# Two edge columns of passes 1 to 3, one of pass 4 and one of the last scatter moved by single-row transfers

## What is computed

```
edge_index = stack([src, dst])
h = relu(layernorm(x)); x = x + RGAT(relu(RGAT(h, W1..)), W2..)   # passes 1 and 2
h = relu(layernorm(x)); x = x + GAT(h)                           # pass 3
h = relu(layernorm(x)); x = x + RGCN(h, edge_weight)             # pass 4
h = relu(layernorm(x)); x = x + GINE(h, edge_attr)               # last layer
# attention: alpha = leaky(q[etype,dst] + k[etype,src]); softmax over the edges of a dst;
#            out[dst] = sum softmax * xw[etype, src]
# GINE:      message[e] = relu(h[dst[e]] + edge_attr[e]); out[src[e]] += message[e]
```

## Time and profile before

| | us |
|---|---|
| median of 3 runs | 36401.83 (36386.37 to 36415.52) |
| profiled execution, span from its first to its last instruction | 22678.7 |
| pass 1, from POOL's first gather to DVE's start on the last chunk | 447 to 4473 |
| pass 2, the same | 4779 to 8740 |
| pass 3, the same | 9049 to 13010 |
| pass 4, POOL's first to last gather | 13248 to 17207 |
| last layer's scatter, POOL's first to last | 17530 to 21634 |

### The profile page before, as it was taken

One profiled execution on the slowest core, in us unless ns is written; L12 is line 12 of the kernel. 1 busy time (PEld: TensorE's weight loads), 2 busy tenths in 40 slices (PEclk: granted clock), 3 DMA queues, 4 the chain that ended last, 5 costly groups with the idle time before them and its releaser, 6 DMA issues.

```text
span 22678.7 us, 201879 instructions
## 1 busy us (share of the span) xinstructions
PE 5315.0 (23%) x30665; PEld 3876.7 (17%) x30665; DVE 10606.0 (47%) x9480; ACT 5421.1 (24%) x4707; POOL 16413.3 (72%) x17069
## 2 busy tenths in 40 slices
PE   2000000020000001222222266666662222222201
PEld 1000000010000001222222255555552000000001
DVE  2444444324444443556566668888884111111167
ACT  1222222222222222111111132222221211121175
POOL 7777777677777776777777767777776777777733
PEclk9999999999999999666666655555555666666655
DMA  6333333332222222222222232222222222222164
GB/s 203 95 98 101 95 98 98 88 97 76 70 75 70 72 73 46 54 54 58 54 57 55 52 87 56 52 56 52 56 52 61 84 76 76 76 80 80 66 235 162
DMA packets 782414, 1839.84 MB, mean 81 GB/s; under 512 B 380834, under 2 KB 415306, under 8 KB 720302
## 3 DMA queue, kind: packets, MB, share of 16 engines
q0 software_dynamic: 544128, 569.36, 13.8%
q10 hardware_dynamic: 88736, 721.35, 8.1%
q1 hardware_dynamic: 148622, 541.43, 6.7%
HBM read 1007.43 MB, written 929.12 MB: 85 GB/s over the span
## 4 chain that ended last, share of the span: by engine, by line
POOL 55%; issue 24%; SPq 12%; DMA 3%; DVE 2%; PE 2%; ACT 1%; POOLq 0%; DVEq 0%; ACTq 0%
POOL region L652 41%; POOL by_src L742 12%; SPq L615 9%; SPq L613 3%; DMA region<-by_src 2%; DMA row_list<-row_lists 1%; POOL q_rel L713 1%; SPq L614 1%; PE ps L1207 1%; DVE region L1567 1%; DVE region L1538 0%; PE ps L1168 0%; POOL h_edge L725 0%; PE ps L1209 0%; POOL q_one L713 0%
## 5 line engine op out<-in xcount | busy, mean ns | idle before, releaser
L652 POOL DMA_INDIRECT region<-table,idx x12688 | 11972.1, 944 | 3941.9 <-issue 3873.2
L742 POOL DMA_INDIRECT by_src<-region,idx x3224 | 3122.7, 969 | 1007.9 <-issue 1001.5
L1950 DVE TENSOR_TENSOR region<-ps,region 128x248 f32<-128x248 f32 (+1 forms) x156 | 74.4, 477 | 3958.0 <-DMA region<-table,idx 1967.5
L1216 PE MATMUL ps<-ident,region 128*68 128x128 f32 (+1 forms) x3 | 1.3, 444 | 8044.9 <-DVE region L2013 8044.9
L1767 DVE TENSOR_TENSOR region<-ps,region 128x2048 bf16<-128x2048 f32 x833 | 1845.8, 2216 | 18.2 <-DVE region L1761 8.0
L870 ACT COPY region<-region 128x4216 f32<-128x4216 f32 (+1 forms) x156 | 1182.2, 7579 | 2477.7 <-DVE region L1996 2477.7
L1112 PE MATMUL ps<-region 98*128 98x128 f32 x6448 | 1657.9, 438 | 323.3 <-DVEq L1833 192.8
L1533 DVE CAST region<-src 128x62 f32 (+1 forms) x52 | 11.7, 224 | 3463.8 <-DMA by_src<-region,idx 3463.6
L1207 PE MATMUL ps<-region,ident 128*128 128x512 f32 (+1 forms) x832 | 809.5, 1062 | 3141.2 <-DVE region L1538 3141.2
L1112 PEld LDWEIGHTS ps<-region 98*128 98x128 f32 x6448 | 1455.9, 330 | 410.7 <-DVEq L1833 269.7
L1905 DVE TENSOR_TENSOR_SCAN region<-region,ps 128x1008 f32<-128x1008 f32 x624 | 1382.9, 2244 | 10.7
(11 more groups left out here) (291 smaller groups left out, 16216.1 us busy)
## 6 DMA issues: line engine op xcount, KB each, us to landing
sums<-region ACTq DMA_DIRECT2D x104, 2232.0 KB
region<-table SPq DMA_DIRECT2D x13312, 0.3 KB
sums<-region ACTq DMA_DIRECT2D x104, 1984.0 KB, 11.1
region<-table,idx POOLq DMA_INDIRECT x12688
region<-table SPq DMA_DIRECT2D x6656, 0.3 KB
region<-table SPq DMA_DIRECT2D x6656, 0.2 KB
sums<-region ACTq DMA_DIRECT2D x52, 2046.0 KB
region<-by_src SPq DMA_DIRECT2D x52, 2015.0 KB, 9.6
```

Of the source, the lines that this page charges most:

```text
L652: pool.indirect_dma_start(out=to, out_offset=None, in_=table, in_offset=bass.IndirectOffsetOnAxis(ap=index, axis=0)).then_inc(s, 16)
L742: pool.indirect_dma_start(out=by_src, out_offset=bass.IndirectOffsetOnAxis(ap=idx[:, b, j:j + 1], axis=0), in_=MSG[:, b, j, :], in_offset= ...
```

## The change

- In passes 1 to 3 the last **two** columns of each chunk (256 rows) go by single rows, and POOL gathers 60. SP fetches rows 0 to 143 of these 256, ACT rows 144 to 255, from a function `fetch_rows` of its own. ACT does so inside `score_chunk` for the chunk after the one that it works on: it asks for its part of the list at the start, fetches 80 rows after the mask at line 1001 and before its wait for the scores, and 32 rows after the exponentials and before `store_sums`. All 112 rows of the first chunk come before the loop.
- Pass 4 keeps one column by rows, by SP alone, and 61 by POOL.
- The lists hold byte offsets instead of row numbers (DVE multiplies them once, near the start), and the row DMAs are addressed in bytes (`U8`), so that no register instruction is left between two of them. 32 registers are loaded at a time (`RUN`), not 16. SP asks for the lists of both chunks of a turn at its start.
- The zeros over `h_edge` are written in quarters, one in each of the four passes, after each chunk.
- In the last layer POOL scatters 61 columns; SP stores the 128 rows of column 62, one DMA each, with row numbers that are written to DRAM as `rank_lists` when the layer begins. These keep the register instruction. SP does this between its loads: the loads of chunk c+1 come before the rows of chunk c.

```diff
+ROWED = {0: 2, 1: 2, 2: 2, 3: 1}
-RUN = 16
+RUN = 32
+SP_ROWS = 144
+FEWER = 32
+GROUPS_2 = [(0, 64), (64, 128), (128, SP_ROWS), (SP_ROWS, 208), (208, ROWS)]
...
@@ sync, at the start (one column of src and of edge_type before)
+            for j in range(2):
+                sp.dma_start(list_src[:, of], a["src"].rearrange(...)[:, :, J - 2 + j]).then_inc(loaded, 16)
+                sp.dma_start(list_type[:, of], a["edge_type_8"].rearrange(...)[:, :, J - 2 + j]).then_inc(loaded, 16)
...
@@ sync, last layer
+                    def load_edges(i, b):
+                        sp.wait_ge(he_t, i * 8 + (4 * b + 4))
+                        sp.dma_start(HE[...], he[...]).then_inc(he_in[b], 16)
+                        sp.wait_ge(edge_sum, i * (2 * NS) + (NS * b + 1))
+                        sp.dma_start(EA[...], ea[...]).then_inc(ea_in, 16)
+                    def send_rows(i, b, back):
+                        nth = b - 2 * back
+                        sp.dma_start(row_list[b:b + 1, 0:P], rank_lists[bass.ds(i * 2 + nth, 1), :]).then_inc(list_in[b], 16)
+                        sp.wait_ge(idx_ready, i * 2 + ((CH + 2) * len(SUMMED) + nth + 1))
+                        sp.wait_ge(xs_ready, i * (2 * NS) + (NS * nth + NS + 2))
+                        sp.wait_ge(list_in[b], i * 16 + 16 * (CH // 2 * len(SUMMED) + 1 - back))
+                        for p0 in range(0, P, RUN):
+                            sp.load(indices, row_list[b:b + 1, p0:p0 + RUN])
+                            for k, row in enumerate([sp.snap(r) for r in indices]):
+                                p = p0 + k
+                                sp.dma_start(by_src[bass.ds(row, 1), :], MSG[p:p + 1, b, J - 1, :]).then_inc(msg_rows[b][p // 64], 16)
+                    load_edges(0, 0)
+                    sp.dma_start(rank_lists.rearrange("c p -> p c"), src8[:, J - 1:EPP:J]).then_inc(lists_out, 16)
+                    sp.wait_ge(lists_out, 64)
+                    load_edges(0, 1)
+                    send_rows(0, 0, 0)
+                    with sp.Fori(1, CH // 2) as i:
+                        load_edges(i, 0)
+                        send_rows(i, 1, 1)
+                        load_edges(i, 1)
+                        send_rows(i, 0, 0)
+                    send_rows(CH // 2, 1, 1)
...
@@ sync, passes 1 to 4
+                mine = (0, SP_ROWS) if ROWED[l] == 2 else (P, ROWS)
...
+                        for k0 in range(mine[0], mine[1], RUN):
+                            n = min(RUN, mine[1] - k0)
+                            sp.load(indices[0:n], row_list[b:b + 1, k0:k0 + n])
+                            for k, row in enumerate([sp.snap(r) for r in indices[0:n]]):
+                                sp.dma_start(row_place(l, b, k0 + k), row_bytes(l, row)).then_inc(...)
-                        if l == CONV1:
-                            sp.dma_start(he[:, bass.ds(i * (2 * J * D) + b * J * D, J * D)], zeros_d).then_inc(big_zero, 16)
+                        w = J * D // QUARTERS
+                        sp.dma_start(he[:, bass.ds(i * (2 * J * D) + (b * J * D + l * w), w)], zeros_d[:, 0:w]).then_inc(big_zero, 16)
...
@@ gpsimd
-                            for j in range(J):
+                            for j in range(J - 1):
...
-                        for j in range(JP):
+                        for j in range(gathered_columns(l)):
...
@@ scalar, passes 1 to 3
+                    ask_rows(0, 0)
+                    rows_begin(0, 0)
+                    fetch_between(0, SP_ROWS, ROWS)
...
+                        if more:
+                            ask_rows(i + b if b else i, 1 - b)
                         act.copy(EQT, EQ.rearrange("p j k -> p k j")).then_inc(e_read, 1)
...
                         act.copy(REP[:, 0:k, 1:J1], bc(cont[:, bass.ds(at, J)], 1, k)).then_inc(q_in, 1)
+                        if more:
+                            rows_begin(i + b if b else i, 1 - b)
+                            fetch_between(1 - b, SP_ROWS, ROWS - FEWER)
                         act.wait_ge(ex_in, i * 2 + nth)
...
+                        if more:
+                            fetch_between(1 - b, ROWS - FEWER, ROWS)
                         store_sums(i, b, O)
...
@@ scalar and vector, last layer, before a chunk's MSG is overwritten
-                            dve.wait_ge(scat[b], i * (16 * J))
+                            dve.wait_ge(scat[b], i * (16 * (J - 1)))
+                            for half in range(2):
+                                dve.wait_ge(msg_rows[b][half], i * (16 * 64))
```

More of the change, by code:

```diff
@@ L502, in piece, with row_place, row_bytes, gathered_columns @@
             return slice(q * PF, (q + 1) * PF)
+        lists = wide[0:CH].rearrange("p a b -> p (a b)").bitcast(I32)
+        list_src, list_type = lists[:, 0:ROWS], lists[:, ROWS:2 * ROWS]
+        def row_place(l, b, k):
+            j, p = divmod(k, P)
+            return slots(l)[1][p:p + 1, b, J - 1 + j, :].bitcast(U8)
+        def row_bytes(l, at):
+            n = 4 * row_in(l)
+            return tables[l].bitcast(U8).rearrange("n f -> (n f)")[bass.ds(at, n)].unsqueeze(0)
+        def gathered_columns(l):
+            return J - ROWED[l]
+        def row_groups(l):
+            return GROUPS_2 if ROWED[l] == 2 else GROUPS_1
+        def row_group(l, k):
+            return [lo <= k < hi for lo, hi in row_groups(l)].index(True)
         block = ctx.enter_context(nc.Block())
@@ L778, in _ @@
         def _(act):
-            steps = Steps(act, act_s)
+            act_indices = [act.alloc_register(f"act_row{k}") for k in range(RUN)]
             act.sem_inc(free_a, 2)
@@ L875, in _, with ask_rows, rows_begin, fetch_rows @@
                 sum_rows = sums[l].rearrange("(p j) f -> p j f", p=P) if l in SUMMED else None
+                def ask_rows(i, b):
+                    act.dma_start(row_list[b:b + 1, SP_ROWS:ROWS],
+                                  row_lists[bass.ds(i * 2 + (CH * ROW_KIND[l] + b), 1), SP_ROWS:ROWS]).then_inc(act_list_in, 16)
+                def rows_begin(i, b):
+                    act.wait_ge(idx_ready, i * 2 + ((CH + 2) * l + b + 1))
+                    act.sem_inc(chunk_begun, 1)
+                    act.wait_ge(act_list_in, i * 32 + 16 * (CH * l + b + 1))
+                    act.sem_inc(chunk_begun, 1)
+                def fetch_rows(b, k0, n):
+                    act.load(act_indices[0:n], row_list[b:b + 1, k0:k0 + n])
+                    for k, row in enumerate([act.snap(r) for r in act_indices[0:n]]):
+                        act.dma_start(row_place(l, b, k0 + k), row_bytes(l, row)).then_inc(rows_in[b][row_group(l, k0 + k)], 16)
+                def fetch_between(b, k0, k1):
+                    for k in range(k0, k1, RUN):
+                        fetch_rows(b, k, min(RUN, k1 - k))
+                if l in SUMMED:
+                    for q in range(GP):
+                        act.wait_ge(stored[q], 16 * TURNS * (l + 1))
+                    if l == CONV1:
+                        act.wait_ge(lists_out, 48)
                 def send_sums(i, b, O):
@@ L982, in edge_chunks @@
                     if not first:
-                        act.wait_ge(scat[b], i * (16 * J))
+                        act.wait_ge(scat[b], i * (16 * (J - 1)))
+                        for half in range(2):
+                            act.wait_ge(msg_rows[b][half], i * (16 * 64))
                     for k in range(NS):
@@ L1576, in sorted_sums @@
                 for b in range(2):
-                    dve.wait_ge(scat[b], 16 * J * (CH // 2))
+                    dve.wait_ge(scat[b], 16 * (J - 1) * (CH // 2))
+                    for half in range(2):
+                        dve.wait_ge(msg_rows[b][half], 16 * 64 * (CH // 2))
                 done(dve.memset(SOT[:, :, J:J1], 0.0))
@@ L1720, in _ @@
                 nth = l
+                if l:
+                    for b in range(2):
+                        for part in range(len(GROUPS_2)):
+                            dve.sem_clear(rows_in[b][part])
                 if l == RGCN:
@@ L1848, in piece_step @@
                             if q == 0:
-                                dve.wait_ge(gathered[l][b], i * (16 * JP) + 16 * JP)
-                                for half in range(2):
-                                    dve.wait_ge(rows_in[l][b][half], i * (8 * P) + 8 * P)
+                                dve.wait_ge(gathered[l][b], i * (16 * gathered_columns(l)) + 16 * gathered_columns(l))
+                                for part, (lo, hi) in enumerate(row_groups(l)):
+                                    dve.wait_ge(rows_in[b][part], i * (16 * (hi - lo)) + 16 * (hi - lo))
                             elif not ranks:
```

93 lines of the change are left out of this document (55 added, 38 removed).

## The result

| | before | after |
|---|---|---|
| median of 4 runs, us | 36395.41 (36386.37 to 36415.52) | 37796.52 (37791.25 to 37804.18) |
| ratio, 95% interval | | 1.038 (1.037 to 1.040) |
| span of the profiled execution, us | 22678.7 (see below) | 37791.1 |

The change makes the kernel slower by 3.8%. The profiled execution of the changed kernel took 37,792.9 us by the clock of the runs, so its span is its time less 1.8 us: nothing lies outside the span. The rows ahead of the prediction have to be read with one reservation: the trace of before shows an execution of 22,679 us, and no timed run of that kernel, then or later, was shorter than 36,223 us. The kernel before was therefore profiled once more (experiment e1), and after is compared with that trace, whose span is 36,237.0 us.

What follows compares the result with a forecast made beforehand. POOL's transfers were taken to bound passes 2 to 4 and the last scatter, SP pass 1. Terms -125 - 65 - 65 + 134 + 8 = -113 us on 36,402 gave 36,289 us; range 36,060 to 36,520.

Steps and rivals of the forecast that it cites:

- The step that failed: Whole kernel: of the 36,402 us median, 13,723 us outside the 22,679 us span were taken as unchanged.
- The rival on the time outside the span: Whole kernel: timed runs longer in proportion (1.605), POOL still bounding the last layer, 507 us gained, 35,895 us; chance 0.10.
- The rival of dearer rows: Last layer: SP's rows cost more and lose more than the passes gain, 36,490 to 36,616 us; chance 0.15.
- Passes 1 to 3: One POOL gather less a chunk: 65 us off each pass, and 60 more off pass 1 as SP leaves the path.
- Pass 4: POOL keeps 61 gathers, so nothing changes.
- Last layer: SP's turn of 81.55 us, 65.1 of it rows, never catches up with POOL's 77.7: 134 us lost.
- Sizes: Single instructions on SP and ACT: a row DMA 0.225 us on SP, a load of 32 registers 2.2 us.
- Start: Ahead of POOL's first gather: two more list loads on SP cost 8 us.
- Signs: Trace marks: right if POOL's gathers come 1.25 us apart without pause and it pauses once a chunk in the last layer.
- ACT's exponentials 2 us late chunk after chunk: Passes 1 to 3: forecast wrong if exponentials begin later than 2 us after DVE's scores, chunk after chunk.
- 81 to 82: Last layer: forecast right if POOL pauses once a chunk, 81 to 82 us apart; wrong if it has no pause.

Runs made afterwards that it cites:

- e1: The kernel before, unchanged, profiled once more: time 36,238.7 us, span 36,237.0 us.
- e8: The changed kernel with a small POOL iota and a wait for it behind every second transfer, in passes and last layer's scatter: 28,708.3 us, ratio 0.792.
- e6: The kernel before with a small POOL iota and a wait for it behind every second gather of the passes: 28,111 us.
- e12: The kernel before with a small POOL iota and a wait for it behind every sixth gather of the passes: 34,673 us.
- e2: The kernel before without any single-row DMA in the passes, POOL gathering all 62 columns: 29,739.0 us, ratio 0.820.
- e14: The kernel before without single-row DMAs in the passes, with a small POOL iota and wait behind every eighth gather: 29,704.8 us.
- e13: The kernel before without single-row DMAs in the passes, with a small POOL iota and wait behind every fourth gather: 27,751.8 us, ratio 0.763.
- e10: The kernel before, its gathers fetching rows for partitions 0 to 63 only from the third chunk of each pass on: 36,447.3 us.

## Why the prediction was wrong

- **The step that failed** is the first one: "13,723 us of it are in no row. I take them as unchanged." The argument rested on a trace in which rows lie beside POOL's gathers, while in the kernel as timed most of them stand behind them (e1). The number hinted at it: 13,723 us over 208 chunks are 66.0 us, and a chunk's rows are 67.1. (By e1, 59.8 us a chunk lie in the passes; the rest is in the last scatter, 390 us longer, and elsewhere.) Had I put that in place of "outside the span", the prediction's own estimates would have given passes 1 to 3 as one gather less and rows of 60.5 us instead of 67.1 (-65 - 343 each), pass 4 as rows of 53.6 (-702) and the last layer as 52 x 65.1 - 66 (+3,319): with the start 37,803 us, against 37,797. That the sum comes this near is chance: the parts would still have been off, pass 1 by 236 and pass 4 by 555 us. The sign comes from the last layer alone.
- **The rival on the time outside the span** had half of it (the timed runs are longer, not offset) and priced it wrongly: it stretched everything in proportion, so POOL stayed the bound and the last layer gained. POOL's gathers did not stretch (946 ns against 944), its last scatter by a tenth (4,497 us against 4,107).
- **The rival of dearer rows** had the sign and the place, rows of the last layer that cost more than the passes gain. It took 71.4 us a chunk as the most, by a dearer store and a dearer load. Neither is what happened: a store's instruction has a median of 224 ns, and beside POOL the rows took 130 us.
- **Passes 1 to 3** (-65 each, and 60 more in pass 1): the mechanism forecast, POOL nearly without pause, is what e8 shows, with 76 to 89 us. In the changed kernel POOL pauses in every chunk; most of the gain of 372 to 644 us is a shorter pause, and one gather less is 65 of it. Pass 1 did gain more than pass 2, 272 us and not 60: in e1 it is 266 us longer than pass 2, in after as long. That the zeros and the list do it, as forecast, no run tests by itself.
- **Pass 4** (0): -147 us, with room +14. Its rows lost their register instruction, which would shorten the pause; that is argued, not shown.
- **Last layer** (+134): +3,017. SP did come late in the form that was forecast: both loads are 0.57 us apart, its wait for the list ends 11.6 us behind the first (13.5 in the sum), and it never catches up. The mis-sized term is the rows, 130 us instead of 65.1: the sum let them lie beside POOL's scatter at the speed of the earlier trace rows. Where POOL leaves room they take 62 (e8).
- **Sizes.** Those of a single instruction hold. Row DMAs of SP and ACT have medians of 225 and 235 ns, and a load of 32 registers takes 2.07 us on SP, 2.15 on ACT and 2.11 in the last layer (2.2 estimated). The Trainium skill's 200 ns a register ("Runtime: NRT & Kernel Launch", "Instruction fetch mechanics"), which would make it 6.4 us, does not hold in these rows:

```profile
L681 SPq TENSOR_LOAD <-row_list x988: 3/2067/5971, 550.3 to 28685.3; - x198
L958 ACTq TENSOR_LOAD <-row_list x624: 691/2151/2334, 553.0 to 21229.3; - x156
L630 SPq TENSOR_LOAD <-row_list x208: 657/2112/2283, 29067.2 to 36651.9; - x104
```

- **Start** (+8): POOL's first gather is at 546.6 us, in e1 at 530.4: +16.
- **Signs.** POOL pauses in passes 1 to 3, which speaks against the forecast. The sign that was named for being wrong, ACT's exponentials 2 us late chunk after chunk, did not come in passes 1 and 2: there they begin 35 ns behind DVE's scores in the median, and are over 2 us late in 12 of some 100 chunks. It came in pass 3, where ACT was said to have more room: 7.4 us late in the median, 0.03 in e1. In the last layer the turn is 147 us and not 81 to 82.

## What to carry to other kernels

Before a trace is used, hold its span against the timed runs; where they differ, the trace is of another regime, and the difference divided by the number of turns can hint at which work changed its place. Whether two engines' work overlaps has to be seen in the rows of both (here the duration of a register move, 29 or 700 ns), not inferred from their using different queues. And an engine that transfers at its highest rate may cost the others more than it gains: with a small rest behind every second or third transfer this kernel took 22 to 27% less time.

## What the runs showed of the hardware

- While POOL issued an indirect DMA every 1.25 us, nearly every instruction of SP or ACT, register moves included, came to take 0.70 us (e1, after), and POOL's own gathers kept their 0.94. At a mean pitch of 1.58 us hardly anything was slowed (e6); at 1.36 POOL stood for some 46 us a chunk again (e12).
- POOL does not keep up 1.25 us either where nothing makes it pause. In the stages that have hardly a pause its transfers came 1.39 us apart in the mean: passes 1 and 2 of e2, with 65 to 69 instructions of the others a chunk, and the last scatter of e1 (4,496.6 us for 3,224). Only the first trace of before shows 1.25 and 1.27 throughout. The rests of e12 and e14 would have made 1.36 and 1.33 us, below that; those of e13 1.42.
- It builds up, and runs down. POOL resumes at 16,081.8 in e1; SP's moves in the 5 us after it, then from 5 to 15, then from 15 to 25 us:

```profile
L615 SPq MOVE region<-table x14: 29/29/29, 16079.3 to 16086.6; - x14
L615 SPq MOVE region<-table x8: 2/29/1385, 16087.3 to 16095.9; - x8
L615 SPq MOVE region<-table x4: 687/694/1385, 16095.9 to 16105.6; - x4
```

  After POOL's last gather of a chunk (16,156.8) SP's instructions go on at 0.70 us until 16,167.2 and are then at full speed.

- It goes by transfers or packets, not bytes (e10), which leaves what comes once for each: the semaphore updates, the completions, the packets themselves, or the records of these. The records are affected too: counted in the traces, that of before holds 338,175 semaphore updates by DMAs, that of the same kernel in e1 87,642. Releasers are inferred from these records, so those named in e1 and the runs like it, "unknown queue" above all, are less sure than in the first trace. The Trainium skill ("NOTIFIC — the notification-queue block", section "7.1 Overflow: three behaviours, one of which stalls the engine") says that the block which writes such records holds its producers back rather than lose one inside. No run here shows whether that held SP, or the updates themselves did. That, and why the first trace of before is free of the slowing, stays open.
